# One of sixteen state terms of a Mamba scan added to y by VectorE in place of ScalarE, a buffer and a transfer

## The reference, cut to what matters

```
s[d, n] = s[d, n] * exp(delta[d] * A[d, n]) + delta[d] * u[d] * B[n]
y[d]    = sum over n of s[d, n] * C[n]        (then + u[d] * D[d])
out     = (y * silu(z)) @ out_proj
```

## Time and profile before

| | |
|---|---|
| median of three runs | 2781.83 us |
| time of the profiled execution | 2781.71 us |
| its span in the trace | 2779.9 us |
| busy in the span: PE, DVE, ACT, POOL | 86%, 85%, 71%, 82% |
| granted TensorE clock, mean | 0.921 of full speed |
| DMA with addition into `y_sb` | 384, of 388.85 MB of traffic in all 201.35 MB on their queue |
| steady part | POOL's `y_gate` of the first chunk starts at 231.5 us, of the last at 2669.3 us |

### The profile page before, as it was taken

How to read it: one execution, slowest core, us unless ns; L and a number is a source line. 1 busy time by engine, 2 the same in 40 slices (tenths; PEclk the granted TensorE clock), 3 DMA queues, 4 the chain that set the end, 5 groups by cost and what they waited for, 6 DMA issues and landing times.

```text
span 2779.9 us, 51800 instructions
## 1 busy us (share of the span) xinstructions
PE 2395.2 (86%) x16084; PEld 1915.6 (69%) x16084; DVE 2360.0 (85%) x3751; ACT 1977.6 (71%) x3777; POOL 2280.8 (82%) x2254
## 2 busy tenths in 40 slices
PE   4557989989798898979989798988989898898989
PEld 1334777768677686867768586776868677686867
DVE  4888989898898989889898898889888898988853
ACT  4786877778677777867677786777778777786631
POOL 2777898979889798988979899797988979798942
PEclk7658999989899998999999999999989999899999
DMA  2575666757567575665757565674756667476731
GB/s 84 159 161 111 142 152 142 166 121 161 121 146 169 126 165 129 146 144 139 160 121 175 135 140 132 155 169 111 165 128 145 142 151 160 114 161 147 159 85 56
DMA packets 136128, 388.85 MB, mean 140 GB/s; under 512 B 20232, under 2 KB 22920, under 8 KB 135600
## 3 DMA queue, kind: packets, MB, share of 16 engines
q0 software_dynamic: 55296, 201.35, 39.1%
q1 hardware_dynamic: 80560, 184.20, 20.7%
HBM read 166.29 MB, written 17.87 MB: 66 GB/s over the span
## 4 chain that ended last, share of the span: by engine, by line
PE 32%; POOL 26%; issue 18%; DVE 10%; ACT 8%; DMA 3%; POOLq 0%; DVEq 0%; ACTq 0%; SPq 0%
PE bank_ps L1469 13%; POOL db_sb L711 12%; PE moe_ps L1487 7%; PE rows_ps L1405 6%; DVE states L1194 4%; POOL act L754 4%; POOL y_sb L723 3%; POOL y_sb L732 2%; PE bank_ps L1353 2%; POOL du_sb L698 2%; ACT da_ps L955 2%; PE bank_ps L1365 2%; DMA y_sb<-c_rows 2%; DVE c_rows L1236 1%; ACT c_rows L928 1%
## 5 line engine op out<-in xcount | busy, mean ns | idle before, releaser
L711 POOL TENSOR_TENSOR db_sb<-du_sb,b_sb 128x512 f32<-128x512 f32 x1024 | 1498.5, 1696 | 33.4 <-DVE states L1194 33.3
L955 ACT ACTIVATE da_ps<-delta,a_sb 128x512 f32<-128x512 f32 x1024 | 704.9, 692 | 136.1 <-DVE states L1194 132.4
L1405 PE MATMUL rows_ps<-ident,states 128*128 128x128 f32 x4096 | 627.8, 291 | 142.2 <-DVE states L1194 102.4
L1469 PE MATMUL bank_ps<-h2T_high,ein_w_high 128*128 128x256 f16 x2304 | 646.6, 281 | 49.8 <-DVE delta L1168 20.7
L754 POOL TENSOR_TENSOR act<-act,w_sb 128x256 f32<-128x256 f32 x512 | 506.3, 1142 | 206.8 <-DVE act L1291 184.0
L1405 PEld LDWEIGHTS rows_ps<-ident,states 128*128 128x128 f32 x4096 | 509.4, 150 | 236.9 <-DVE states L1194 113.3
L1194 DVE TENSOR_TENSOR_SCAN states<-da_ps,carry,db_sb 128x512 f32<-128x512 f32 x512 | 648.1, 1276 | 5.2 <-ACT da_ps L955 3.1
L1469 PE MATMUL bank_ps<-h2T_high,ein_w_low 128*128 128x256 f16 x2304 | 645.5, 280 | 0.0
L1469 PE MATMUL bank_ps<-h2T_low,ein_w_high 128*128 128x256 f16 x2304 | 644.4, 280 | 0.0
L1194 DVE TENSOR_TENSOR_SCAN states<-da_ps,db_sb 128x512 f32<-128x512 f32 x512 | 616.6, 1216 | 13.3 <-ACT da_ps L955 12.5
L1487 PE MATMUL moe_ps<-eout_sb,act 128*128 128x256 f32 x2304 | 577.9, 384 | 10.9 <-POOL act L754 10.8
(11 more groups left out here) (169 smaller groups left out, 2685.6 us busy)
## 6 DMA issues: line engine op xcount, KB each, us to landing
y_sb<-c_rows POOLq DMA_DIRECT2D x384, 512.0 KB, 5.3
b_sb<-b_dram SPq DMA_DIRECT2D x128, 512.0 KB, 5.2
w_sb<-w_dram SPq DMA_DIRECT2D x256, 256.0 KB, 3.6
th_p<-x_dram SPq DMA_DIRECT2D x16, 512.0 KB, 5.3
r_dram<-conv SPq DMA_DIRECT2D x16, 512.0 KB, 5.0
x<-r_dram SPq DMA_DIRECT2D x16, 512.0 KB, 3.7
out_dram<-x SPq DMA_DIRECT2D x32, 256.0 KB, 5.5
mod_p<-mod_dram SPq DMA_DIRECT2D x7, 384.0 KB, 4.4
```

What stands on the lines that cost most here:

```text
L711: pool.tensor_tensor(db_sb[:, n % NDB, :], du_sb[:, slots[t][0][0], b, :], b_sb[:, k % NBPAIR, s % BPAIR, :], ALU.mult).then_inc(sem["scal ...
L955: ac.activation(da_ps[n % NDA][:, :], delta[:, slots[t][0][0], b, :], ACT.Exp, scale=a_sb[:, b, s:s + 1]).then_inc(sem["exp_done"], 1)
L1405: last = pe.transpose(rows_ps[j % 2][:, b * P:b * P + P], states[:, step % 2 * NB + b, j * P:j * P + P], ident[:, :])
L1469: last = pe.matmul(bank(key)[:, a * HALF:a * HALF + HALF], ein_w16[w][:, k, e // 2, at:at + HID], h2T[h][:, k, q * HALF:q * HALF + HALF], ...
```

## The change

Every chunk's last state (s = 15, `NS - 1`) no longer goes through `c_rows`. A new DVE step `y_join` reads `rows_ps`, multiplies by C and adds to `y_sb` in place. It waits for the rows and for the DMA that added state 14 to the same pair of j. State 15 has no `c_scale` and no `c_add` any more, and `y_gate` waits for `y_join` in place of the last DMA. The wait of `rows` for its PSUM tile becomes a wait for `y_join` where the rows before belong to state 15. The counts that other waits use (`c_scales`, `piece`) follow. Beside it all constants of the due times were searched anew, so the order of all steps can differ. In the diff below the tables are cut to the entries that the text speaks of.

```diff
-            out.append((at + 0.145, ("c_join" if s in JOINED else "c_scale", t, s, j)))
-            if j % CPAIR == CPAIR - 1 and s + 1 not in JOINED:
+            out.append((at + 0.145, ("y_join" if s == NS - 1 else "c_join" if s in JOINED else "c_scale", t, s, j)))
+            if j % CPAIR == CPAIR - 1 and s + 1 not in JOINED and s < NS - 1:
                 out.append((at + 0.892, ("c_add", t, s, j // CPAIR)))
...
-LEAD_P0, LEAD_P, LEAD_M = 9.4848, 7.9681, 36.993
-TICK, ROUTED, UNITS_END = 1.4006, 15.946, 63.7625
-Z_AHEAD, Y_SOON, Y_LATE = -0.3185, 22.219, -0.2513
-SLOT = 70.0828
+LEAD_P0, LEAD_P, LEAD_M = 9.9027, 7.976, 54.2167
+TICK, ROUTED, UNITS_END = 1.4174, 15.9402, 63.6971
+Z_AHEAD, Y_SOON, Y_LATE = -0.0663, 27.652, -0.8495
+SLOT = 70.5212
...
             def c_scales(step, j):
                 k, s = divmod(step, NS)
-                joins = len(JOINED) * k + sum(q < s for q in JOINED)
+                joins = sum(q < s for q in JOINED)
+                if s == NS - 1:
+                    return sem["y_joined"], NJ * k + j + 1
                 if s in JOINED:
-                    return sem["c_joined"], NJ * joins + j + 1
-                return sem["c_scaled"], NJ * (step - joins) + j + 1
+                    return sem["c_joined"], NJ * (len(JOINED) * k + joins) + j + 1
+                return sem["c_scaled"], NJ * ((NS - 1 - len(JOINED)) * k + s - joins) + j + 1
...
                         if nS(t):
-                            pool.wait_ge(*c_adds(piece(nS(t) * NS - 1, j)))
+                            pool.wait_ge(*c_scales(nS(t) * NS - 1, j))
                         place = y_sb[:, slots[t][2][0], j, :]
                         pool.tensor_tensor(place, place, zg[:, j % 2, :], ALU.mult).then_inc(sem["y_gated"], 1)
...
+                    def y_join(t, s, j):
+
+                        step = NS * nS(t) + s
+                        place = y_sb[:, slots[t][0][0], j, :]
+                        v.wait_ge(sem["rows_full"], NJ * step + j + 1)
+                        v.wait_ge(*c_adds(piece(step - 1, j)))
+                        v.scalar_tensor_tensor(place, rows_ps[j % 2][:, :], xd_sb[:, slots[t][0][0], j, s:s + 1], place,
+                                               ALU.mult, ALU.add).then_inc(sem["y_joined"], 1)
```

More of the change, by code:

```diff
@@ L138, in mix_steps @@
     return out
-LEAD_P0, LEAD_P, LEAD_M = 9.4848, 7.9681, 36.993
-TICK, ROUTED, UNITS_END = 1.4006, 15.946, 63.7625
-SOFT = 45.4792
-Z_AHEAD, Y_SOON, Y_LATE = -0.3185, 22.219, -0.2513
-SLOT = 70.0828
[L146 to L160, removed]
@@ L250 @@
[L250 to L252 removed]
+LEAD_P0, LEAD_P, LEAD_M = 9.9027, 7.976, 54.2167
+TICK, ROUTED, UNITS_END = 1.4174, 15.9402, 63.6971
+SOFT = 45.451
+Z_AHEAD, Y_SOON, Y_LATE = -0.0663, 27.652, -0.8495
@@ new lines @@
+SLOT = 70.5212
+SHIFT = {"a_made": -21.027, "b_load": -2.722, "b_store": 8.448, "c_add": 1.455, "c_join": 0.351, "c_scale": 0.747, "carry": 0.648,
+         "constants": 18.022, "ct_silu": 2.289, "ct_tanh": 14.625, "delta": -0.277, "dt_bias": -0.563, "dt_high": -0.518, "dt_low": -2.154,
+         "dtp": 0.354, "du": -2.417, "e_act": -0.159, "e_mul": -0.069, "e_tanh": -0.43, "e_weigh": 1.026, "ein_high": -14.859,
+         "ein_load": -6.811, "ein_low": 4.19, "eout_fold": -17.224, "eout_load": 31.095, "exp": 1.094, "expert_in": -0.102,
+         "expert_out": 0.777, "first_loads": -9.603, "fold": -8.275, "gather": 0.59, "h2_high": 0.53, "h2_low": -0.106, "h2_scale": -0.301,
+         "h2_t": 2.244, "h_rms": -2.353, "h_scale": 0.361, "h_square": 1.004, "hn_high": 0.042, "hn_low": 2.391, "hn_t": -0.717,
+         "in_high": 3.135, "in_low": -8.168, "logit": -1.438, "logit_exp": 1.435, "mod0": -10.582, "mod0_gate": 17.753, "mod0_rows": 1.336,
+         "mod_m_load": 7.053, "mod_p_load": -8.4, "mod_rows": 20.647, "mod_store": -4.481, "mods": -3.635, "norm_lift": -5.942,
+         "op": 1.413, "op_gate": 1.314, "out_add": 1.058, "out_gate": 0.083, "out_scale": 5.203, "out_store": 3.16, "r_add": 6.222,
+         "r_gate": 0.685, "r_load": 4.276, "r_store": 14.224, "router": 1.665, "rows": 0.237, "scaled": 0.647, "scan": -0.094,
+         "skip": -0.951, "skip_evac": 0.828, "skip_t": -0.107, "soft_exp": -1.274, "soft_ln": 0.561, "tap": 0.07, "u": -0.787,
+         "u_tanh": -0.176, "w_evac": -0.283, "w_load": -0.677, "w_store": 3.81, "w_t": -0.559, "x1": 0.908, "x1_norm": -1.065,
+         "x1_rstd": -2.012, "x1_stat": 0.812, "x_load": -3.059, "x_norm": 1.782, "x_rstd": 2.345, "x_scale": -0.679, "x_shift": -1.036,
+         "x_stat": -0.805, "xd": -1.055, "xd_evac": 0.057, "xd_t": 0.025, "xd_t_evac": -1.809, "xi": 0.102, "xi_center": 0.032,
+         "xi_copy": 0.042, "y_evac": 0.74, "y_gate": 0.207, "y_join": 0.227, "y_t": 0.952, "z": -2.232, "z_gate": -1.694, "z_tanh": -1.323}
@@ L255, in place @@
+START = {"a_made": -8.949, "constants": -7.533, "ct_silu": -16.404, "ct_tanh": -13.749, "first_loads": 27.458, "fold": 1.055,
+         "in_high": 0.627, "in_low": 7.261, "mod0": 3.212, "mod0_gate": 3.313, "mod0_rows": -4.136, "mod_rows": 0.914, "mod_store": 18.312,
+         "mods": -12.286, "norm_lift": 17.868, "out_scale": 1.297}
 def place(what):
-    return "_".join(str(n) for n in (what[0], *(what[3:] if what[0] in ("exp", "scaled", "scan", "rows", "c_scale", "c_join", "c_add") else what[2:])))
+    return "_".join(str(n) for n in (what[0], *(what[3:] if what[0] in ("exp", "scaled", "scan", "rows", "c_scale", "c_join", "y_join", "c_add") else what[2:])))
```

43 lines of the change are left out of this document (20 added, 23 removed), and 140 rows, old and new, of the table PLACE.

## The result

The changed kernel takes 2738.59 us (median of four runs, 2737.5 to 2741.5), the kernel before on the same chip 2782.49. The ratio is 0.9843, interval 0.9829 to 0.9858: 43.9 us or 1.6% faster. The prediction had 2765 and a range down to 2744. Its direction was right, its size was not: the gain is 2.6 times the 16.6 us forecast, and lies outside of the range by 5.4 us.

The account below looks back on a forecast made before the run. No single engine bounds the kernel, but POOL bounds the slot boundary. Of 27.7 us saved there (26.4 plus 1.3), 60% or 16.6 was to pass, with nothing counted for ACT, DVE or new waits: 2765 us, range 2744 to 2792.

Parts of the forecast that it names:

- An issue ... I take 0.88: POOL at the slot boundary: each removed DMA issue saves 0.88 us, 1.76 per boundary, 26.4 over fifteen.
- I take 60%: Behind the boundary, DVE 96% busy: only 60% of POOL's 27.7 us saving passes, 16.6 us.
- the rival at 2750: Boundary saving passes in full, PE idles less and keeps its clock: 27.7 us and a few more; chance 0.20.
- It fits, but narrowly: DVE at the boundary: 2.97 us of y_join fits its idle times with 1.4 us left; bounds nothing or 47.5 us.
- The rival that DVE becomes the bound: DVE's added 47.5 us counts in full against POOL's 27.7: slower, 2801.5, half-way 2789; chance 0.16.
- ACT: I count nothing: 64 c_scale removed from ACT, 44.0 us, among idle time off the chain: nothing counted, 3.5 us gain if uncovered.
- The new waits: y_join's wait for state 14's DMA and the rows at the boundary: nothing counted, up to 2 us a boundary kept.
- The rival that the transfer's wait takes the place of the issue: y_join waits for state 14's landing, blocking DVE and PE: 28 us cancels the gain, 2782; chance 0.10.
- One sign that the prediction named as showing it wrong: Waits for DVE's scans (ACT's exp, POOL's products) growing by more than 15 us in all.
- At the last one ... that goes, 1.3 us.: Last boundary, POOL idle before the issue: y_gate's 1.29 us wait for the transfer goes, 1.3 us gained.
- The order searched anew ... I can't price: Neighbouring steps' due times, moved mostly under a unit: effect unpriced, range widened 0.3%, about 8 us each side.
- The busy-share rule beside it: Steady part: DVE has the largest share of engines other than PE, so moving work from POOL to DVE goes wrong.

Follow-up runs that it names:

- e9: Changed kernel with state 15's two POOL issues put back as plain 512 KB transfers to spare memory, each pair with its own semaphore and place: 2759.60 us.
- e14: Kernel before, old due times, state 15's two issues left out, its c_scale writing a spare tile never added, no work given to DVE: 2744.26 us.
- e13: Changed kernel in which ACT also keeps an instruction of c_scale's size at state 15's places, from constants to a spare tile: 2744.39 us.
- e15: Kernel before on the new due times, state 15's two issues left out, its c_scale writing a spare tile, no work given to DVE: 2736.12 us.
- e1: Changed kernel's code on the due times of the kernel before, y_join standing where c_scale of state 15 stood: 2791.98 us.
- e6: Changed kernel with every y_join done a second time with factor 0: 2781.48 us.
- e7: Changed kernel's code on the old due times, with y_join behind the statistics, last expert products ahead of the rows, first two z gates moved: 2789.64 us.
- e8: Changed kernel's code on the old due times, with only y_join behind the statistics and the last expert products ahead of the rows: 2798.46 us.
- e11: Changed kernel with only y_join due half a unit to a unit (2.3 us) earlier: 2785.42 us.
- e10: Changed kernel with state 13 taken back from DVE to ACT and POOL, with 32 issues and their transfers more: 2817.07 us.

## Why the prediction was wrong in size

**"An issue ... I take 0.88", bounds 0.60 and 1.08.** Mis-sized. In the string the two issues took 2.09 us, 1.04 each, near the upper bound. An issue itself had 0.92; the rest was the wait of 0.24 us in front of one of them, which the earlier trace rows showed and I left out. The string changed by 2.16 us at 14 boundaries (the first gave nothing), 30.2 us, where I had 15 x 1.76 = 26.4. By itself this is a small miss.

**"I take 60%" of it passes.** This is the step that failed. What is taken from the string passes in full: in `e9` 18.6 us of issues cost 18.8 over the same slots with the rest unchanged, and `e14` has a string shorter by 1.88 us with a slot shorter by even more. The row that I weighed against it, DVE busy for 96% behind the boundary, was no reason. My reading is that DVE, ACT and PE get their next inputs earlier by as much as POOL does, so a full engine behind the string moves with it; a busy share would only hold the gain back if that engine had a start of its own that doesn't depend on the string. Passing in full would have given 2754 us, inside of the range; above all it was the rest of the slot, next, that took the result out of it.

**The rest of the slot, 14 x 1.07 = 15.0 us.** It wasn't in the sum; of it I had only the half sentence in the rival at 2750, that PE "keeps its clock". It isn't ACT's relief: with ACT's work back (`e13`) the rest is 134.84. It isn't the issues' time or their traffic either: with plain ones back (`e9`) it is 134.90. It is there when only the issues go (`e14`, 135.34, -0.65) and larger on the new places (`e15`, 134.91). What goes along with it is the granted clock behind the boundary. Windows of before and of after, 20 us each, at the same distance from `x1_rstd` (columns as in the earlier trace rows):

```profile
1394.00:1414.00 20.00, 12.63 (x81) 9.29 (x82) 19.65 (x33) 14.84 (x29) 18.33 (x18) 0.73 0.46 103
1414.00:1434.00 20.00, 19.10 (x130) 15.04 (x129) 19.04 (x34) 14.96 (x32) 11.12 (x11) 0.93 0.68 158
```

```profile
1372.00:1392.00 20.00, 13.92 (x105) 10.59 (x103) 19.54 (x33) 15.64 (x32) 17.57 (x18) 0.83 0.41 94
1392.00:1412.00 20.00, 17.19 (x121) 13.11 (x120) 19.69 (x36) 15.35 (x31) 14.33 (x15) 1.00 0.80 174
```

The clock is a mix of the levels 1.2 and 2.4 GHz. Its mean over 13 slots, in the 20 us ahead of `x1_rstd` and the two stretches of 20 us behind it, is 0.91, 0.76, 0.94 before; 1.00, 0.80, 0.96 after; 1.00, 0.80, 0.98 in `e14`; 0.93, 0.80, 0.97 in `e1`. Over the whole run it is 0.921 before and 0.943 after. Before, PE waited 3.10 us for `y_gate` and its clock fell earlier.

Such means leave the cause open, but single slots settle most of it. In `e14` the order is that of before. In one stretch, 15 to 24 us behind `x1_rstd`, the granted clock is 0.62 in 11 of the 13 slots before and in 3 of 13 in `e14`; in all others it is 0.81. Here are two slots of one execution of `e14`, the fourth and the sixth (columns as in the earlier trace rows), and what DVE does at the end of the stretch in the sixth:

```profile
747.16:756.16 9.00, 6.71 (x37) 4.49 (x38) 8.52 (x25) 5.85 (x12) 4.30 (x5) 0.81 0.63 139
1068.61:1077.61 9.00, 7.25 (x32) 4.79 (x33) 7.89 (x24) 4.63 (x9) 3.13 (x3) 0.62 0.62 138
```

```profile
1077.78 0.42 DVE L1292 SCALAR_TENSOR_TENSOR act<-act,bank_ps 128x256 f32<-128x256 f32 x1 [0.79 <-ACT act L1028]
```

Where PE stays at the lower level longer, its products come late, then ACT's `act`, and DVE waits for it: 0.5 to 0.9 us in each of those 14 slots and in no other of the two kernels. The rest of the sixth slot is 135.30 us, of the fourth 133.94. By every second slot, as they alternate, the rest is 133.94 to 134.27 and 135.85 to 136.21 at 0.81, and 135.12 to 135.44 and 136.45 to 137.04 at 0.62: about 1 us more. Eight such slots fewer are the whole 0.65 us of `e14`. If no slot had it, before would have some 135.1 (an estimate from `e14`'s slots at 0.81), which leaves 0.2 of the 1.07 to the new places; the changed kernel has none of these waits. So most of this term is PE's clock. What is not shown is why the level returns later in those slots, and no run changed the clock alone. The means over all kernels don't order the rest: on the new places it is 134.8 to 134.9 in `e13` and `e9`, whose clocks just behind `x1_rstd` are 0.77 and 0.83.

**"It fits, but narrowly" (DVE's new work, counted nothing).** Right for the changed kernel, and with no spare at all: `y_join` costs 2.5 to 4.4 us net there (`e15` to after; 8.3 if ACT's load is held equal, `e15` to `e13`, half of it at the first boundary), and a second one costs 42.9 of 44.2 us (`e6`). But I had put it down to room in DVE's idle time, and it is the order that makes it fit: in the old order the same work costs 47.7 us. The rival that DVE becomes the bound is true of `e1`, `e7`, `e8` and `e11`, not of this kernel.

**"ACT: I count nothing", 3.5 us at most.** Small, but not nothing: 5.8 us between `e13` and after (3.9 by the differences to before), 0.43 us a boundary in the string.

**The new waits, "I count nothing for it".** Right for the transfer: 1.2 us at one `y_join` of 64. The rival that the transfer's wait takes the place of the issue is what the old order gives (`e1`: 21.9 us in 16 waits). One sign that the prediction named as showing it wrong did appear: ACT's waits for DVE's scans grew by 35.8 us, from 132.4 to 168.2, and POOL's did not (33.3 to 32.2). It was a bad sign to choose. `e15`, the fastest kernel of all, has 168.1 us without any `y_join`, and `e1` has 138.5 with it: these waits go with the new places, on an engine that has room.

**"At the last one ... that goes, 1.3 us."** Wrong in sign. The last slot is 1.3 us longer, since with POOL idle `y_gate` now waits for `y_join` and the z gate.

**"The order searched anew ... I can't price", 8 us on each side.** This bound failed by much, and is the other reason why the range missed. Order and edit can't be priced apart: alone +13 us and +8 us, together -44. Treating the order as a small symmetric error lost what it does, which is to find a place for `y_join` that delays neither the statistics nor the z gates. `e11` shows how sharp that place is. What could have been read ahead of the result is the place itself, from the due times: behind the statistics and between the z gates.

**The rival "passes in full, clock kept" (2750)** was the right mechanism, with 0.20. Its sum, with 1.04 for 0.88 and 1.07 us a slot for "a few more", is 14 x 2.16 + 14 x 1.07 - 1.3 = 43.9 us, which is what was measured. These terms were read from the two traces afterwards, so the sum shows where the gain is and is no second test of it.

**The busy-share rule beside it.** By the Trainium skill (Perfetto Trace Analysis, section Identifying the Most-Contended Engine) the engine with the highest occupancy is to be optimized first. Taken over the steady part, the runs don't bear that out here: loading DVE, the fullest of the three engines other than PE, further gave 1.6%, and relieving it at a place off the string, `e10`, cost 78 us. Issues, transfers and ACT's scalings came back with it; which of them costs the most wasn't taken apart. Taken over the boundary alone the same measure names POOL, 19.50 of 20 us, and there the trace agrees.

## What to carry to other kernels

When a chain of waits stands on one in-order engine without a gap at the boundary of every iteration, price what is removed from it at its whole length, its own small waits with it, and let it pass in full; a busy share of 96% on the engines behind it was no discount here, where they are fed by that chain. Work added to another engine cost next to nothing or all of itself, according to what stands right behind it in that engine's queue: name the readers that are due next, here the statistics and the z gates, and look whether the new step comes behind them. An edit and the order made for it are one change: tried on the old order, a good edit can look like a loss.
